# Attention scores in a Trainium2 kernel: two 64-row fp32 tiles on queries moved by DMA, or four 32-row tiles on queries used in place

## The reference, cut to what matters

```
q = (hs @ wq.T).reshape(b, s, 32, 64)          # 32 query heads of 64
k = (hs @ wk.T).reshape(b, s, 8, 64)           # 8 key heads, each used by 4 query heads
q, k = x * cos + rotate_half(x) * sin          # the two halves of 32 of each head are mixed
scores = einsum('bhqd,bhkd->bhqk', q, k) / 8   # causal mask, softmax
o = einsum('bhqk,bhkd->bhqd', probs, v)
x = x + o @ wo.T
```

## Time and profile before

| | |
|---|---|
| median of 3 runs | 865.78 us (865.48 to 867.25) |
| the profiled execution's own time | 865.23 us |
| its span in the trace | 863.3 us |
| attention, about | 0 to 560 us |
| routing, about | 560 to 641 us |
| experts, about | 641 to 863 us |

### The profile page before, as it was taken

How to read it: one execution, slowest core, us unless ns; L and a number is a source line. 1 busy time by engine, 2 the same in 40 slices (tenths; PEclk the granted TensorE clock), 3 DMA queues, 4 the chain that set the end, 5 groups by cost and what they waited for, 6 DMA issues and landing times. The chain is left out here.

```text
span 863.3 us, 18994 instructions
## 1 busy us (share of the span) xinstructions
PE 764.6 (89%) x5895; PEld 640.0 (74%) x5895; DVE 492.0 (57%) x1943; ACT 487.9 (57%) x1537; POOL 459.0 (53%) x690
## 2 busy tenths in 40 slices
PE   3589999999999999999999999936019999999994
PEld 3478888888888888888888888722017888888883
DVE  5777667567576566676666666555962333333331
ACT  1477877777777777777777777825212223222221
POOL 1356565565665665655656556527642445554442
PEclk9799999999999999999999999977559999999998
DMA  6343121211212212212212112038651223333230
GB/s 194 105 126 101 42 56 45 62 50 51 60 45 59 56 36 71 50 39 74 51 38 68 57 38 65 23 115 265 174 190 28 50 44 49 49 52 55 42 56 2
DMA packets 51905, 61.16 MB, mean 71 GB/s; under 512 B 10368, under 2 KB 45440, under 8 KB 51552
## 3 DMA queue, kind: packets, MB, share of 16 engines
q1 hardware_dynamic: 40144, 48.48, 19.6%
q0 software_dynamic: 7488, 9.36, 6.7%
q10 hardware_dynamic: 4176, 2.11, 0.9%
HBM read 26.34 MB, written 9.32 MB: 41 GB/s over the span
## 5 line engine op out<-in xcount | busy, mean ns | idle before, releaser
L794 POOL TENSOR_SCALAR probs<-exps,inv_sums 128x128 f32<-128x128 f32 x256 | 96.0, 375 | 213.8 <-DVE inv_sums L660 159.5
L543 ACT COPY pT<-probsT 128x384 f32<-128x384 f32 x256 | 122.7, 479 | 77.6 <-PE probsT L424 77.5
L424 PE MATMUL probsT<-tables,probs 128*128 128x128 f32 x768 | 132.5, 282 | 8.9 <-POOL probs L795 7.4
L534 ACT ACTIVATE exps<-masked,neg_max 128x128 f32<-128x128 f32 x256 | 103.2, 403 | 46.7 <-DVE neg_max L654 46.0
L536 ACT ACTIVATE exps<-masked,neg_max 128x256 f32<-128x256 f32 x256 | 127.4, 498 | 0.0
L795 POOL TENSOR_SCALAR probs<-exps,inv_sums 128x256 f32<-128x256 f32 x256 | 124.8, 487 | 0.0
L1387 POOL DMA_INDIRECT out<-y,to_token x39 | 61.9, 1587 | 101.8 <-DVE y L1356 79.5
L652 DVE CUSTOM_DVE_ANT_0 masked<-scores,tables 128x128 f32<-128x128 f32 x256 | 71.8, 281 | 76.8 <-PE scores L411 64.1
L424 PEld LDWEIGHTS probsT<-tables,probs 128*128 128x128 f32 x768 | 84.1, 141 | 32.7 <-POOL probs L795 17.2
L654 DVE CUSTOM_DVE_ANT_0 masked<-scores,tables 128x256 f32<-128x256 f32 x256 | 107.4, 419 | 0.0
L411 PE MATMUL scores<-kT,qT 64*128 64x128 f32 (+1 forms) x1024 | 102.8, 341 | 3.9 <-DMA qT<-rotated 3.9
(11 more groups left out here) (150 smaller groups left out, 1818.3 us busy)
## 6 DMA issues: line engine op xcount, KB each, us to landing
qT<-rotated SPq DMA_DIRECT2D x256, 64.0 KB, 2.2
kT<-k_cos SPq DMA_DIRECT2D x64, 128.0 KB, 3.4
experts_w_out<-w_in SPq DMA_DIRECT2D x16, 512.0 KB, 4.5
raw<-w_attn SPq DMA_DIRECT2D x20, 256.0 KB, 3.0
experts_w_out<-w_out SPq DMA_DIRECT2D x2, 2048.0 KB, 10.0
out<-x_all SPq DMA_DIRECT2D x8, 256.0 KB, 2.3
xn_rows<-experts_w_out ACTq DMA_DIRECT2D x4, 512.0 KB, 5.1
x_all<-x SPq DMA_DIRECT2D x1, 1792.0 KB, 10.7
```

The source lines that it names most:

```text
L424: mm = nc.tensor.transpose(p_bank[:, at:at + P], probs[:, h, at:at + P], ident)
L534: nc.scalar.activation(exps[:, h, 0:P], masked[:, h, 0:P], ACT.Exp, bias=neg_max[:, h, 0:1], scale=-1.0, accum_out=sums[:, h, 0:1])
L543: nc.scalar.copy(pT[:, n % 2, h, :], p_bank[:, 0:3 * P]).then_inc(pT_done, 1)
L794: nc.gpsimd.tensor_scalar(probs[:, h, 0:P], exps[:, h, 0:P], inv_sums[:, h, 0:1], 1.0, ALU.mult, ALU.mult)
```

## The change

The queries are no longer moved. The columns of the query weights are put into another order on the host, so that the projection leaves partition p = 32 head + d, and the rotated queries already stand with 32 partitions for each head, the two rotary halves side by side in `rotated`. The scores of a head are the sum of two products of 32 rows, one for each rotary half, added up in PSUM. So a turn has 16 matmuls of 32 rows in place of 8 of 64, and they are issued by tile, half and head, the four heads lying in four different groups of 32 rows of the array. The keys are copied to four groups of partitions, both halves side by side: four DMAs of 256 KB for each half batch in place of four of 128 KB. The tables have separate cosines and sines for queries and keys (960 KB in place of 576 KB). `move_q`, `qT` and the semaphores `q_in` are gone. `scores` waits for all four `maxima` of the last turn before it starts, and `s_ps` rises once, by 4, after the last matmul; the wait in `maxima` stays as it was.

```
-ATTN_TABLE = 3 * SEQ + 3 * P
+ATTN_TABLE = 6 * SEQ + 3 * P
...
-    qT = sb("qT", [P, 2, PAIRS, SEQ])
-    kT = sb("kT", [P, 2, HALF, SEQ])
+    kT = sb("kT", [P, 2, HALF, 2, SEQ])
...
-        def move_q(m, s, first=False):
-
-            sp.wait_ge(q_rotated, m + 1)
-            if not first:
-
-                sp.wait_ge(s_ps, (m - 1) * GROUP)
-            for odd in range(2):
-                for a in range(2):
-                    at = odd * HD + a * 32
-                    sp.dma_start(qT[at:at + 32, s, :, :], rotated[odd:P:2, s, a, :]).then_inc(q_in[s], 16)
...
-            for a in range(2):
-                for copy in range(2):
-                    at = copy * HD + a * 32
-                    sp.dma_start(kT[at:at + 32, half, :, :], k_cos[:, a, :]).then_inc(k_in[half], 16)
+            for h in range(GROUP):
+                sp.dma_start(kT[h * 32:h * 32 + 32, half, :, :, :], k_cos[:, :, :]).then_inc(k_in[half], 16)
...
-            pe.wait_ge(q_in[g % 2], (n // 2 + 1) * 64)
+            pe.wait_ge(q_rotated, n + 1)
             if g % HALF == 0:
                 pe.wait_ge(k_in[g // HALF], b * 64 + 64)
-            for pair in range(PAIRS):
-                if n > 0:
-
-                    pe.wait_ge(s_read, (n - 1) * GROUP + 2 * pair + 2)
-                for tt in range(TT):
-                    for odd in range(2):
-                        rows = slice(odd * HD, odd * HD + HD)
-                        mm = nc.tensor.matmul(s_bank[2 * pair + odd][:, tt * SEQ:tt * SEQ + (tt + 1) * P],
-                                              qT[rows, g % 2, pair, tt * P:(tt + 1) * P],
-                                              kT[rows, g // HALF, g % HALF, 0:(tt + 1) * P], start=True, stop=True)
-                mm.then_inc(s_ps, 2)
+            if n > 0:
+
+                pe.wait_ge(s_read, n * GROUP)
+            for tt in range(TT):
+                for a in range(2):
+                    for h in range(GROUP):
+                        rows = slice(h * 32, h * 32 + 32)
+                        mm = nc.tensor.matmul(s_bank[h][:, tt * SEQ:tt * SEQ + (tt + 1) * P],
+                                              rotated[rows, n % 2, a, tt * P:(tt + 1) * P],
+                                              kT[rows, g // HALF, g % HALF, a, 0:(tt + 1) * P],
+                                              start=(a == 0), stop=(a == 1))
+            mm.then_inc(s_ps, GROUP)
...
             pool.wait_ge(q_parts, m + 1)
             if not first:
-                pool.wait_ge(q_in[m % 2], m // 2 * 64)
+                pool.wait_ge(s_ps, (m - 1) * GROUP)
...
-    wqT = wq.T.reshape(KT, P, KV_HEADS, GROUP, 2, HD // 2).transpose(1, 2, 0, 4, 5, 3).reshape(P, KV_HEADS, PIECE_COLS)
+    wqT = wq.T.reshape(KT, P, KV_HEADS, GROUP, 2, HD // 2).transpose(1, 2, 0, 4, 3, 5).reshape(P, KV_HEADS, PIECE_COLS)
```

More of the change, by code:

```diff
@@ L79, in shape_constants @@
     cos, sin = np.cos(ang).astype(np.float32), np.sin(ang).astype(np.float32)
-    cosT, sinT = np.repeat(cos.T, GROUP, 0), np.repeat(sin.T, GROUP, 0)
+    cos_q, sin_q = np.tile(cos.T, (GROUP, 1)), np.tile(sin.T, (GROUP, 1))
+    cos_k, sin_k = np.repeat(cos.T, HALF, 0), np.repeat(sin.T, HALF, 0)
     q, k = np.arange(P)[:, None], np.arange(P)[None, :]
@@ L85, in shape_constants @@
     ones = np.ones((P, P), np.float32)
-    attn = np.concatenate([cosT, -sinT, sinT, mask, ident], 1)
+    attn = np.concatenate([cos_q, -sin_q, sin_q, cos_k, -sin_k, sin_k, mask, ident], 1)
     rev = np.tile(EXPERTS - np.arange(EXPERTS, dtype=np.float32), TILES)
@@ L109, in attention @@
     tables = sb("tables", [P, ATTN_TABLE])
[L110 to L113, removed]
+    cos_q = tables[:, 0:SEQ].rearrange("p (o t) -> p o t", o=1).to_broadcast([P, 2, SEQ])
+    sin_q = tables[:, SEQ:3 * SEQ].rearrange("p (a t) -> p a t", a=2)
+    cos_k = tables[:, 3 * SEQ:4 * SEQ].rearrange("p (o t) -> p o t", o=1).to_broadcast([P, 2, SEQ])
+    sin_k = tables[:, 4 * SEQ:6 * SEQ].rearrange("p (a t) -> p a t", a=2)
+    mask = tables[:, 6 * SEQ:6 * SEQ + 2 * P]
+    ident = tables[:, 6 * SEQ + 2 * P:6 * SEQ + 3 * P]
     raw = sb("raw", [P, SLOTS, PIECE_COLS])
@@ L174, in attention @@
     v_done = sem("v_done")
-    q_in = [sem("q_in0"), sem("q_in1")]
     k_in = [sem("k_in0"), sem("k_in1")]
@@ L265, in turn @@
                 move_k(b + 1, 0)
-            if prepares(b, g):
-                move_q(turn_of(b, g) + 2, g % 2)
             if g == 3 and b > 0:
@@ L289, in _ @@
         load_piece(SLOTS + 1)
-        move_q(0, 0, True)
-        move_q(1, 1, True)
         for i in range(SLOTS + 2, SLOTS + EARLY):
@@ L295, in _ @@
         for s in range(2):
-            sp.wait_ge(q_in[s], 64 * (TURNS // 2))
             sp.wait_ge(k_in[s], 64 * BATCH)
@@ L629, in rope_q @@
             halves = x_bank[:, :].rearrange("p (a t) -> p a t", a=2)
-            nc.vector.tensor_tensor(by_cos[:, :, :], halves, cos, ALU.mult)
-            nc.vector.tensor_tensor(by_sin[:, :, :], halves[:, ::-1, :], sin, ALU.mult).then_inc(q_parts, 1)
+            nc.vector.tensor_tensor(by_cos[:, :, :], halves, cos_q, ALU.mult)
+            nc.vector.tensor_tensor(by_sin[:, :, :], halves[:, ::-1, :], sin_q, ALU.mult).then_inc(q_parts, 1)
         def rope_k(b, half):
@@ L640, in rope_k @@
             halves = x_bank[:, :].rearrange("p (a t) -> p a t", a=2)
-            nc.vector.tensor_tensor(k_cos[:, :, :], halves, cos, ALU.mult)
-            nc.vector.tensor_tensor(k_sin[:, :, :], halves[:, ::-1, :], sin, ALU.mult).then_inc(k_parts, 1)
+            nc.vector.tensor_tensor(k_cos[:, :, :], halves, cos_k, ALU.mult)
+            nc.vector.tensor_tensor(k_sin[:, :, :], halves[:, ::-1, :], sin_k, ALU.mult).then_inc(k_parts, 1)
         def maxima(b, g, h):
@@ L915, in _ @@
         sp.dma_start(consts[:, :], t["route_consts"]).then_inc(consts_in, 16)
-        sp.dma_start(ident[:, :], t["attn_consts"][:, 3 * SEQ + 2 * P:]).then_inc(consts_in, 16)
+        sp.dma_start(ident[:, :], t["attn_consts"][:, 6 * SEQ + 2 * P:]).then_inc(consts_in, 16)
         sp.dma_start(gate[:, :, :], t["gate"].rearrange("p (k e) -> p k e", k=KT)).then_inc(consts_in, 16)
@@ L1227, in _ @@
     def _(sp):
-        sp.dma_start(ident[:, :], t["attn_consts"][:, 3 * SEQ + 2 * P:]).then_inc(ident_in, 16)
+        sp.dma_start(ident[:, :], t["attn_consts"][:, 6 * SEQ + 2 * P:]).then_inc(ident_in, 16)
         for p in range(RING):
```

## The result

The kernel after takes 881.06 us (median of 4 runs, 879.3 to 881.27), beside 865.84 us for the kernel before on the same chip: a ratio of 1.0163, 95% interval 1.0141 to 1.0185. It is slower by 15.2 us; the forecast was 875.8, slower by 10.0. The profiled execution took 881.03 us.

| stretch | before, us | after, us | difference | forecast |
|---|---|---|---|---|
| start to the second scores (turn 0 included) | 39.95 | 43.00 | +3.05 | 0 |
| turns 1 to 7 of the first sequence | 61.34 | 63.26 | +1.92 | 1.85 |
| six full sequences | 396.32 | 403.60 | +7.28 | 6.9 |
| last sequence, to its last scores | 55.06 | 56.02 | +0.96 | 0.9 |
| from there to the end of the span | 310.6 | 313.2 | +2.6 | 0.4 |

What follows compares the result with a forecast made beforehand. It took TensorE, busy 89%, as the bound. Stalls behind the late first `maxima` (3.9 + 4.6 + 0.8 + 0.7 = 10.0 us) on the profiled 865.23, plus 0.55 to the median, gave 875.8 us; range 869 to 904, own case 67%.

Steps and rivals of the forecast that it cites:

- The block: TensorE's scores matmuls of one turn: four row groups run side by side, so it stays at 1.51 us, cost 0.
- The late `maxima`: VectorE's first `maxima` of a turn starts 0.66 us later, about 1.8 us after the scores' start in place of 1.15.
- Plain turns: Turns not following a keys projection: idle gaps on ScalarE, VectorE and GpSimd absorb the shift, cost 0.
- Turn 2: Keys were projected the turn before: the projection waits for the late `rope_k`, 0.49 us in each of 8, 3.9 us.
- turn 5: Short turn after a keys projection: it grows by the whole shift, 0.66 us in each of 7, 4.6 us.
- The second chain of turn 5: GpSimd's divides and `rotate_k`, gapless up to the turn's last transposes: this chain moves by the whole 0.66 us.
- Last two turns: No `next_q` between transposes, so head 3's wait for ScalarE's copy: 0.40 us each, 0.8 us.
- The larger tables: In the start-up queue ahead of the weights: TensorE and VectorE could start later; taken as 0, bound +1 us.
- the keys' copies: Keys' transfers with twice the bytes: started more than a turn before their use, so cost 0.
- The second (loads bind, 904): Rival: weight loads or issue bind the scores block, 0.44 us longer each, 904 us; chance 13%.
- third (960): Rival: only two row groups at a time, or strict order, in the scores block, 84 us more, 960 us; chance 7%.
- The fourth and fifth: Rivals: same, late start absorbed or block shorter, about 866 us, 5%; faster, freer TensorE reads shrink the block, 861 us, 8%.

Runs made afterwards that it cites:

- number 1: Kernel after with the keys' rotary products (`rope_k`) placed ahead of the turn's first `maxima` in VectorE's list: 871.94 us, 1.0093.
- number 3: Kernel before with one edit: the scores' semaphore rises once, by 4, after all eight matmuls, in place of by 2 after each pair: 876.05 us, 1.0132.
- both edits: `rope_k` ahead of the first `maxima`, and weight pieces 4 and 5 loaded ahead of the keys' first copy; here put into the kernel before: 863.84 us, 1.0000.
- number 8: Kernel after run and profiled once more, unchanged: 879.18 us, 1.0172.
- number 2: Kernel after with the loads of weight pieces 4 and 5 issued ahead of the keys' first copy: 876.49 us, 1.0156.
- number 5: Kernel after with `rope_k` ahead of the first `maxima` and weight pieces 4 and 5 ahead of the keys' first copy: 870.34 us, 1.0070.
- number 7: Kernel before with each keys' copy made a second time into a tile that nobody reads: 871.08 us, 1.0089.
- number 6: Kernel before with `rope_k` ahead of the first `maxima` and weight pieces 4 and 5 ahead of the keys' first copy: 863.84 us, 1.0000.
- number 4: Kernel after with the head as outermost loop of the scores, so each row group's matmuls stand together: 980.0 us, 1.1343.
- number 9: Kernel after with the scores of each head waiting only for that head's `maxima` of the last turn: 879.87 us, 1.0181.
- Number 10: Kernel after with `rope_k` ahead of the `maxima`, weight pieces 4 and 5 ahead of the keys' first copy, and scores waiting head by head: 869.13 us, 1.0054.
- number 12: Kernel before with `rope_k` ahead of the `maxima`, weight pieces 4 and 5 ahead of the keys' first copy, and one late scores signal: 866.89 us, 1.0002.

## Why the prediction was right, and where it was off

**Right, step by step.** The block: forecast 1.51, measured 1.52; the row with two groups in flight spoke for four. The late `maxima`: 1.8 forecast, 1.84 measured. Plain turns: 0 forecast, 0 to 0.03 measured, so the gaps did take the shift up: in the same turn after, ScalarE's idle 0.26 and 0.39 are gone, and the 0.70 before its next copy stands as before. Turn 2: 0.49 forecast, 0.50 measured; turn 5: 0.66 forecast, 0.63 measured, and numbers 1 and 3 show the cause from both sides. The second chain of turn 5, by GpSimd's divides, is in the trace: beside the 0.46 before the projection, the last transposes' load waits 0.27 for a divide, which it did not before.

Last two turns: 0.8 forecast; they took 0.31 and 0.31 more. The larger tables: 0, bound +1; the first weight piece was rounded at 7.05 us, before at 7.09. First sequence from turn 1 on: 1.85 forecast, 1.92 measured, and this agreement is luck. The parts do not match: turn 1 took 0.70 more, as forecast, but turn 2 took 0.84 less (9.42 for 10.26, though its projection did wait its 0.46), turn 5 only 0.24 more, and turns 3 and 7, forecast at 0, took 0.59 and 0.88 more. The kernel before lost time there itself (61.34, and 59.66 with both edits), and the kernel after gave 64.44 in number 8.

Two readings in the prediction are not quite right, and change nothing in its sum. The two waits for `qT`, 8.0 us, are one wait at 26.11, counted for the weight load and for the matmul. And the low end of its range, 869 or 870, comes from no term: the lowest case it adds up is +7, 873.

**The step that failed** is that about the keys' copies: "The keys' transfers carry twice the bytes, in the same number; they are started more than a turn before their use, so 0 too." It holds for 15 of the 16 copies: the scores waited for `kT` once, at the start. The first is used as soon as it lands, and two weight pieces stand behind it. This term was put at 0. It measured 2.9 us between the kernel after (43.00) and number 2 (40.08), and 2.0 between numbers 8 and 5 (43.40, 41.37), two executions with the slow projection; doubled bytes alone made piece 4 late in number 7. How much it costs depends on when VectorE would have come without it: by the starts of the first `maxima` under number 2 anything from 1.6 to 4.5. The question could have been asked from what was at hand: the change says 256 KB in place of 128 KB a transfer, and the list of SyncE has `move_k(0, 0)` ahead of two `load_piece`. I followed the queries' wait to its end and did not ask who else waits on the queue that the keys' larger copy fills.

**Small terms.** The block's 0.01 and up to 0.03 in single turns add about 0.1 us a sequence: numbers 5 and 6 differ by 0.8 us in the six full sequences (396.79 against 396.00), so about 1 us in all.

**The rivals.** The second (loads bind, 904) and third (960) were excluded by the block of 1.52. Number 4 shows that a slower block was one loop order away, at 980. The Trainium skill's sentence (TensorE: Matmul & The Clock Gate, Part 3, What overlaps and what doesn't) on starts strictly in program order does not agree with number 4 either: by it the block would be 4.6 to 5.3 us (the estimate of number 4), and it is 3.17. The fourth and fifth, same and faster, would have needed a block shorter by 0.16 or more.

**What stays open.** After the last scores the kernel after lost another 2.6 us in its first profile, of which 0.3 is the last turn. The other 2.3 come in routing and the experts (+13.5 us at the end of attention, +15.4 at the first expert, +15.8 at the end), and they belong to that execution and not to the change: in number 8, the same kernel, the gap is +15.2 at the end of attention and +15.8 at the end, and in numbers 2 and 9, which keep `rope_k` where it was, the stretch took 310.5 and 311.2. Over all the traces it takes 308.9 to 312.2 with the kernel before and its variants and 310.5 to 313.3 with the kernel after and its variants. What in routing moves by 2 to 3 us stays open. So of the gap of 15.2 us some 8 are the stalls behind the late signal and 2 to 3 the late piece. The other 4 to 5 (an estimate, the rest of the sum) fall in the first sequence, the small terms, the last turns and this stretch, in other shares in each execution.

Number 10 stays 0.54% behind, 4.7 us. About 1 us of it are the small terms, and 0.7 the last two turns, whose wait for the signal no edit removes (the last sequence 55.44 against 55.06, and 0.3 after the last scores). The late signal in the first sequence would be up to 2.8 (number 12, with its doubt); the rest is unassigned. No kernel tried beat the kernel before by more than the runs can tell.

## What to carry to other kernels

When one signal replaces several, look at what stands behind the waiting instruction in its engine's list, not at the wait: here 60 us more of VectorE's waiting cost nothing in six sequences once `rope_k` had been moved out from behind it, and a signal 0.66 us later in each turn cost 8 us while it stood there. When a transfer grows, check its first use and what is queued behind it apart from the steady state. The largest idle row at a start need not be the one that costs: TensorE's 7 us wait for the keys was worth nothing, and a weight load behind the same copy was worth 2 to 3.

## What the runs showed of the hardware

TensorE kept four groups of 32 rows filled at once when their matmuls were interleaved in program order, and not when they stood group by group: 1.52 us against 3.17, for the same 32 MATMUL instructions and loads.

These copies from SBUF to SBUF, each into 32 partitions, keep the DMA engines busy at a low rate. Four copies of 256 KB, in a window of the first copy and in one of a steady sequence (columns as in rows 2; the last two are DMA share and GB/s):

```profile
20.20:28.20 8.00, 0.94 (x8) 0.73 (x7) 4.36 (x11) 0.00 (x0) 2.19 (x2) 0.82 1.06 136
```

```profile
360.00:364.00 4.00, 4.00 (x45) 3.21 (x38) 2.41 (x14) 2.86 (x11) 2.16 (x6) 1.00 1.05 135
```

At 135 GB/s 1 MB takes 7.8 us with all DMA engines busy, and whatever is queued behind it waits for that. The weight pieces behind the first copy, from DRAM and in packets of 2 KB like the copy's own, moved at 374 to 398 GB/s. The size of the packets does not explain the low rate either: the kernel before copies its keys in packets of 1 KB and reached 153 and 128 GB/s in two windows with the engines as busy (351 to 352 us, share 1.19, and 352 to 353, share 0.93). The time goes with the bytes: 3.4 us to landing for 128 KB, 6.8 for 256 KB. Whether copies into more partitions would be faster, no run tells.
